# A layer norm's inverse deviations sent through DRAM, two VectorE operations in another form, and a new order of steps

## What is computed

```python
h = concat([tokens(x), txt], axis=1)                 # 64 x 193 x 128
h = h + attention(layernorm(h))                      # group norms, 8 heads, relative positions
h = h + ffn(layernorm(h))                            # 8 experts x 512, two gates per token
# layernorm: (x - mean) / sqrt(var + 1e-5) over the 128 channels
# ffn: top-2 probabilities p of softmax(x @ Wg); sum over i of gelu((x * p_i) @ W1) @ W2, plus biases
```

## Time and profile before

| | before |
|---|---|
| median of 3 runs | 3173.65 us (3173.12 to 3177.37) |
| profiled execution, its own time | 3172.15 us |
| its span, first to last instruction | 3170.3 us |
| TensorE matmul busy | 3053.5 us, 96% of the span |
| VectorE / ScalarE / GpSimd busy | 62% / 59% / 46% |
| TensorE's granted clock | 0.99 of full speed |
| DMA | 38 GB/s over the span |

### The profile page before, as it was taken

The page is one execution under the profiler, slowest core; times in us unless marked ns, Lnnn a source line. Parts: engine busy times, 40 slices in busy tenths (PEclk is TensorE's granted clock), DMA queues, the critical chain, the costliest instruction groups (busy, mean ns, idle before and its releaser), DMA issues.

```text
span 3170.3 us, 61793 instructions
## 1 busy us (share of the span) xinstructions
PE 3053.5 (96%) x19776; PEld 2514.4 (79%) x19776; DVE 1951.6 (62%) x4141; ACT 1873.4 (59%) x4370; POOL 1462.0 (46%) x1350
## 2 busy tenths in 40 slices
PE   6986999999999999999999999999999999999998
PEld 5876888777788888777888887778888877788886
DVE  5634566666666666666666666666666666666665
ACT  4642556665555566655565666555655665555557
POOL 1001445555444445554444455544444555544446
PEclk9998999999999999999999999999999999999999
DMA  9971011111110011111100111111101111111010
GB/s 208 224 200 38 18 26 28 28 27 27 26 28 14 20 28 28 28 26 26 28 20 13 28 28 28 26 28 26 27 6 28 28 28 26 28 26 28 4 26 6
DMA packets 92173, 121.58 MB, mean 38 GB/s; under 512 B 8414, under 2 KB 86558, under 8 KB 87710
## 3 DMA queue, kind: packets, MB, share of 16 engines
q1 hardware_dynamic: 87714, 118.24, 15.9%
q10 hardware_dynamic: 4432, 2.99, 0.4%
HBM read 106.23 MB, written 14.97 MB: 38 GB/s over the span
## 4 chain that ended last, share of the span: by engine, by line
PE 73%; DVE 8%; issue 6%; ACT 5%; DMA 0%; POOL 0%; DVEq 0%; ACTq 0%; POOLq 0%; SPq 0%
PE bank L417 14%; PE bank L517 6%; PE bank L426 6%; PE bank L518 6%; PE bank L562 6%; PE bank L563 6%; PE bank L530 6%; PE bank L430 4%; PE bank L427 4%; PE bank L544 3%; PE bank L462 3%; DVE dl L769 3%; DVE gelu L603 2%; ACT gelu L822 2%; PE bank L572 2%
## 5 line engine op out<-in xcount | busy, mean ns | idle before, releaser
L896 POOL TENSOR_TENSOR gelu<-gelu 128x386 f32<-128x386 f32 x1024 | 1077.1, 1073 | 309.6 <-ACT gelu L823 303.2
L822 ACT ACTIVATE gelu<-bank,b_s 128x386 f32<-128x386 f32 x1024 | 593.9, 580 | 644.4 <-DVE gelu L603 628.5
L417 PE MATMUL bank<-gelu,w_s 128*128 128x386 f32 x2048 | 821.0, 487 | 0.3 <-POOL gelu L896 0.3
L603 DVE TENSOR_TENSOR gelu<-bank,ratio 128x386 f32<-128x386 f32 x1024 | 563.6, 557 | 311.6 <-PE bank L430 308.5
L823 ACT ACTIVATE gelu<-gelu,b_s 128x386 f32<-128x386 f32 x1024 | 625.1, 610 | 0.0
L426 PE MATMUL bank<-x_hi,w_hi 128*128 128x386 f32 x1024 | 544.6, 532 | 19.6 <-ACT gelu L822 8.2
L864 ACT ACTIVATE lp<-bank,mx 128x193 f32<-128x193 f32 x800 | 328.6, 425 | 173.8 <-DVE mx L709 173.4
L517 PE MATMUL bank<-k_f,q_bd 128*128 128x193 f32 x1600 | 402.4, 333 | 15.2 <-DVE a_bd L699 8.7
L518 PE MATMUL bank<-rw,a_bd 128*128 128x193 f32 x1600 | 393.4, 328 | 0.0
L417 PEld LDWEIGHTS bank<-gelu,w_s 128*128 128x128 f32 x2048 | 373.1, 189 | 18.5 <-POOL gelu L896 1.2
L909 POOL TENSOR_TENSOR gst<-gst,half 128x4 f32<-128x4 f32 x32 | 32.6, 1018 | 721.0 <-DVE gst L691 721.0
(11 more groups left out here) (131 smaller groups left out, 4575.4 us busy)
## 6 DMA issues: line engine op xcount, KB each, us to landing
a_rep<-u_scratch SPq DMA_DIRECT2D x32, 1600.0 KB, 9.7
xt<-in_x SPq DMA_DIRECT2D x192, 196.0 KB
txt_s<-in_txt SPq DMA_DIRECT2D x32, 128.0 KB, 2.1
u_scratch<-k_f SPq DMA_DIRECT2D x32, 100.0 KB, 2.2
u_scratch<-q_f SPq DMA_DIRECT2D x32, 100.0 KB, 2.2
out<-o_s SPq DMA_DIRECT2D x64, 48.5 KB
out<-o_s SPq DMA_DIRECT2D x64, 48.0 KB
rv<-in_rel_v SPq DMA_DIRECT2D x1, 2624.0 KB, 14.0
```

The lines of the kernel that those rows point to most:

```text
L417: mm(yb[:, 0:T2], w2_s[:, f, :], gelu1[:, f % RING, :], start=(f == 0), stop=(f == NF - 1)).then_inc(S["w2_done"], 1)
L603: v.tensor_tensor(gelu2[:, f % RING, :], zb[f % 2][:, 0:T2], ratio[:, :], ALU.mult).then_inc(S["z2_done"], 1)
L822: a(gelu1[:, f % RING, :], zb[f % 2][:, 0:T2], ACT.Gelu, bias=b1_s[:, f:f + 1]).then_inc(S["g_done"], 1)
L896: g.tensor_tensor(gelu1[:, f % RING, :], gelu1[:, f % RING, :], gelu2[:, f % RING, :], ALU.add).then_inc(S["hs_done"], 1)
```

## The change

`bc1` on TensorE is gone. SyncE sends the four columns of `rs1` to a row `r_scratch` of 388 numbers in DRAM by four DMAs of 97 or 96 numbers, each number from a partition of its own; it waits for them and reads the row back into all 128 partitions of a new tile `r_bc` by a fifth. VectorE multiplies by `r_bc` instead of the bank. The additions in `gate2` and `hres` become `tensor_tensor` with a broadcast operand in SBUF in place of a constant or a per-partition scalar. `SCHEDULE` is reordered.

```diff
-    "c qs0 c qs1 vt am0 qs2 c log0 am1 am2 log1 log2 qs3 hkeep log3 log4 log5 am3 log6 log7 log8 txt log9 mean1 log10 log11 qs4 var1 log12 c tr0 c bc1 c tr1 inv rel0 tr2 rel1 tr3 rel2 tr4 rel3 tr5 rel4 tr6 rel5 rel6 proj pv0 gmean rec0 pv1 gvar rec1 place0 c place1 c omean gaff c ovar c c c c c nqk c c oaff c c onorm c oh2 c c mean2 c c var2 c top c c gate c gate2 c c bcast w2t w2t xin w2t nv a a w2t ot a otr ocopy hres"
+    "c c vt qs0 am0 qs1 c c qs2 log0 am1 hkeep log1 qs3 log2 am2 txt log3 log4 log5 log6 am3 log7 log8 log9 log10 mean1 log11 log12 c qs4 var1 tr0 c c tr1 inv rel0 tr2 rel1 tr3 bc1 rel2 tr4 rel3 tr5 rel4 tr6 rel5 rel6 proj c pv0 rec0 gmean pv1 rec1 gvar place0 place1 c omean gaff c ovar c c c c c nqk c c oaff c c onorm c oh2 c c mean2 c c nv var2 top c gate c c gate2 c c bcast w2t w2t xin w2t a w2t ot a a otr hres ocopy"
...
-        half = sb("half", [P, 2])
+        half = sb("half", [P, 3])
...
+        r_bc = sb("r_bc", [P, T2])
...
+            def repeat_rstd(t):
+
+                sp.wait_ge(S["rstd1"], t + 1)
+                for k, (a, b) in enumerate(zip(GO, GO[1:] + [T2])):
+                    sp.dma_start(r_scratch[a:b].unsqueeze(1), rs1[0:b - a, k:k + 1]).then_inc(S["r_out"], 16)
+                sp.wait_ge(S["r_out"], t * 64 + 64)
+                sp.dma_start(r_bc[:, :], r_scratch[0:T2].unsqueeze(0).broadcast_to([P, T2])).then_inc(S["rstd_bc1"], 16)
+
             def spread(t):
+                repeat_rstd(t)
...
-                elif s == "bc1":
-                    pe.wait_ge(S["rstd1"], t + 1)
-                    broadcast(misc, rs1).then_inc(S["rstd_bc1"], 1)
...
-                    dve.wait_ge(S["rstd_bc" + k], t + 1)
-                    v.tensor_tensor(V2(sq), V2(delta), ps[:, 0:T2], ALU.mult).then_inc(S["x" + k], 1)
+                    dve.wait_ge(S["rstd_bc" + k], t * 16 + 16)
+                    v.tensor_tensor(V2(sq), V2(delta), r_bc[:, :], ALU.mult).then_inc(S["x" + k], 1)
...
-                    v.tensor_scalar(dl[0:GW, 4:8], ep[0:GW, 0:4], 1.0, None, ALU.add).then_inc(S["e1_ready"], 1)
+                    v.tensor_tensor(dl[0:GW, 4:8], ep[0:GW, 0:4], half[0:GW, 2:3].broadcast_to([GW, 4]), ALU.add).then_inc(S["e1_ready"], 1)
...
-                    v.tensor_scalar(hres[:, :], h2[:, :], b2x2[:, :], None, ALU.add).then_inc(S["hres_done"], 1)
+                    v.tensor_tensor(hres[:, :], h2[:, :], b2x2[:, :].broadcast_to([P, T2]), ALU.add).then_inc(S["hres_done"], 1)
...
+            v.memset(half[:, 2:3], 1.0)
```

More of the change, by code:

```diff
@@ L249, in _, with fused_block @@
                         nc.vector.tensor_copy(xs[0:ROWS, slot, s:s + QS0, :], steps(slot, s, s + QS0)).then_inc(dve_packed, 1)
-def fused_block(nc, txt, w1, tok_scratch, u_scratch, out, R):
+def fused_block(nc, txt, w1, tok_scratch, u_scratch, r_scratch, out, R):
     with ExitStack() as ctx:
@@ L312, in fused_block @@
         names = """w1_in w1_hi_ready w1_split setup_dve setup_pool setup_act tok_in txt_t h_ready qk_ready v_ready
-            bn mv_ready gmean gspread gvar gve grstd affine_part affine norm q_spread a_spread a_masked u_out log_ready max_done log_done
+            bn mv_ready gmean gspread gvar gve grstd affine_part affine norm q_spread a_spread a_masked u_out r_out log_ready max_done log_done
             vt v_copied tr_ready tr0_copied tr1_copied wm_done pv_done pv_ready inv_part inv_ready rec_done o_part obn omv omean ospread ovar ove orstd oaff_part oaffine
@@ L940, in build @@
     u_scratch = nc.dram_tensor("u_scratch", (2, DK, BH, LP), F32, kind="Internal").ap()
+    r_scratch = nc.dram_tensor("r_scratch", (T2 + 2,), F32, kind="Internal").ap()
     with ExitStack() as ctx:
@@ L943, in build @@
         patch_embed(nc, a, tok_scratch, R)
-        fused_block(nc, a["txt"], a["w1"], tok_scratch, u_scratch, out.rearrange("b l c -> (b l) c"), R)
+        fused_block(nc, a["txt"], a["w1"], tok_scratch, u_scratch, r_scratch, out.rearrange("b l c -> (b l) c"), R)
 def shape_constants(np):
```

## The result

| | before | after |
|---|---|---|
| median | 3174.2 us | 3315.8 us (3315.4 to 3319.3) |
| ratio | | 1.0447, 95% interval 1.0429 to 1.0465 |
| span | 3170.3 us | 3313.6 us |
| TensorE busy | 3053.5 us, 96% | 3054.3 us, 92% |
| granted clock | 0.99 | 0.96 |

The change makes the kernel slower by 4.5%. The forecast was 3115 us, range 3085 to 3155: wrong, and on the other side. The rival of the late DMA trip had named the place.

The account below looks back on a forecast made before the run. TensorE was taken to bound the kernel. Terms of -2.05 us per turn over 30 turns (-61.5), -1.5 for first and last turns and +5.6 for the prologue made -57.4 from 3172.15: forecast 3115 us, range 3085 to 3155.

Parts of the forecast that it names:

- The rival of the late DMA trip: At VectorE's bc1: a slower trip of 15.4 us comes 4.9 us late each turn, +152 us, 3267 us; chance 0.14.
- the trip's price: Spreading rs1 through DRAM: write 5.5 us plus read 2.2, sum 7.7, between 6.2 and 9.3, hidden in steady turns.
- The slack: From ready rs1 to VectorE's bc1: trip free up to 8.7 us, costing TensorE nothing up to an estimated 10.5.
- The slower rival: The rival of the late DMA trip, the only one slower than before: 3267 us, chance 0.14.
- the prologue's trip: In the prologue nothing hides the trip: 7.7 us in place of the old spreading's 2.04, +5.6 us once.
- gate2: Addition as tensor_tensor waits for one GpSimd sum, not three: TensorE's wait ahead of bcast goes, -0.80 us per turn.
- The sign that I had named for it: Sign that the gate2 forecast holds: VectorE's addition takes under 1.2 us, the product behind the reciprocal up to 1.1.
- a rival of 0.11: At gate2: the new addition waits as long as the old one, the 0.80 us stays, 3139 us; chance 0.11.
- hres: VectorE's addition as tensor_tensor: 0.56 us alone, up to 0.98 more behind a sum; +0.1 us per turn.
- The order: Reordered SCHEDULE: -0.35 us after var2, -0.39 among the logits, +0.2 for later exponentials and back-to-back place steps, per turn.
- bc1's matmuls: Eight records on TensorE go whole if the numbers return from DRAM in time: -0.81 us per turn.
- the two waits of the tail: TensorE's waits of 0.80 us ahead of bcast and 0.35 after var2, both expected to go each turn.

Follow-up runs that it names:

- e10: Changed kernel with e7's read from other rows and the scratch row's numbers 512 bytes apart in DRAM; norm computed with other numbers: 3084.8 us, a single execution.
- e7: Changed kernel, but the fifth DMA reads different, earlier written rows of another scratch tensor, one per partition; norm computed with other numbers: 3215.7 us, ratio 1.0124.
- e6: Changed kernel with each of the two columns of 97 numbers sent as DMAs of 96 and 1, six writes instead of four: 3246.0 us, ratio 1.0228.
- e1: Changed kernel with bc1 again by TensorE's four matmuls behind tr3, new order and both tensor_tensor forms kept: 3105.8 us, ratio 0.9782.
- e2: Changed kernel with VectorE's bc1 moved from behind tr3 to between rel5 and rel6, DMA trip untouched: 3122.1 us, ratio 0.9832.
- e4: Kernel before with one edit, the addition in gate2 as tensor_tensor: 3174.9 us, ratio 0.9998.
- e5: Kernel before with the new order alone: both additions scalar, bc1 by TensorE's matmuls behind tr3: 3103.6 us, ratio 0.9777.
- e8: Changed kernel with VectorE's bc1 moved from behind tr3 to between tr6 and rel5: 3097.9 us, ratio 0.9755.
- e12: Kernel before with top moved directly behind var2 and one chunk more between gate and gate2: 3171.2 us, ratio 0.9988.

## Why the prediction was wrong

**The failed step is the trip's price.** I wrote 7.7 us, between 6.2 and 9.3, and called it hidden. It took 15.7 in the median and 16.8 in the turn shown. The write leg was put at 5.5 us, between 4.0 and 7.1, and took 9.2 to 13.3, median 10.9. My high end was the output stores, pieces of 512 bytes; I reasoned that smaller pieces could only be faster. e10 shows that the size was not the point: side by side, 4-byte pieces take three times as long as apart. The read leg was put at 2.2 us like any other landing and took 4.8; e7's 2.4 shows that the source is the cause, be it that the row is shared or that it has just been written. The bounds came from rows of transfers that differ in the very properties that counted, so they bounded nothing.

The Trainium skill (DMA: Bandwidth & Descriptors, Specifications) says that below 512 bytes the DMA reads, modifies and writes back. That would make neighbouring 4-byte writes wait for one another and distant ones not; e6 and e10 fit that, but no row shows the read, so it stays an inference.

**The slack was right.** 8.7 us from the ready deviations to VectorE's slot: measured 8.65. For TensorE I allowed a trip of 10.5 us. It ran out of work 12.5 us after the deviations were ready, and VectorE's queued work puts its restart 1.8 us behind the landing (1528.93 to 1530.74), so that a trip of about 10.7 would have cost it nothing.

**The slower rival had the mechanism and lacked the clock.** I gave it 0.14. It put the trip at 15.4 us against the median of 15.7, in part by luck: it took two equal legs of 6.8 us, and they were 10.9 and 4.8. It put TensorE's standstill at 4.9 us per turn; in the 30 steady turns with a trip its waits at L537 come to 5.0 us each. What it had at nothing is the clock. In the turn shown TensorE stands still for 6.2 us and then runs some 4.2 us at half clock, which loses about half of that; less the 0.86 us of matmuls that are gone this makes 7.4 us, an estimate, and the turn is 7.3 us longer than e1's, 95.34 against 88.03. The clock fell to half at every one of these trips.

Spans of after and e1 differ by 209 us. Between the first and the last `bcast` lie 188 of these, 6.3 us in each of the 30 turns that have a trip; the other 21 lie ahead of the first, in the prologue's trip and the first turn's. e2, in which only the prologue's trip is on the path, puts that at 14.8 us, where I had +5.6. With these terms the sum comes out: 3114.8, less 29 for the order and the forms (below), plus 9 for the prologue, 7 for the first turn and 212 for the 30 turns (188, and the 24 of matmuls that I had credited) make 3314 us, against the profiled execution's 3315.4.

**gate2.** Forecast -0.80 us per turn for the form; it brought nothing (e4). The sign that I had named for it, an addition under 1.2 us, came in the changed kernel all the same, and that is luck: the order did it (e5). The Trainium skill's rule (SBUF — State Buffer, "SBUF: two separate sides"), which I set against one row and left to a rival of 0.11, had the edit right: both forms exclude GpSimd alike, and both take 2665 ns in the median here. How long such a wait lasts is for the rows to say: an operation of 0.17 us waited through three sums in a row. I took one instruction's behaviour at one place as a property of its form.

**hres.** +0.1 us forecast; the forms together cost 2.2 us of 3105, 0.07 us per turn (e1 against e5), within what the intervals tell.

**The order.** Forecast for the order and both forms, with `gate2`'s wait and without `bc1`'s matmuls: 0.80 + 0.35 + 0.39 - 0.2 - 0.1 = 1.24 us per turn. Measured: 90.24 - 88.03 = 2.21 (e1), and 90.24 - 87.96 = 2.28 with the scalar forms (e5). The distances between TensorE's starts, in one steady turn of before and one of e5, say where; with a chunk at its usual 1.18 us this is an estimate. From `var2` to `bcast` before took 9.63 us with six chunks and e5 7.29 with five, a gain of 1.16: the two waits of the tail, as forecast. The logits with `txt` and `mean1` took 17.54 against 17.06, a gain of 0.48 where I had 0.39. From `proj` to `omean`, two chunks in both, it was 10.45 against 10.15: a gain of 0.30 where I had charged 0.2. Up to the first logit e5 takes 0.90 us more with one chunk more, a gain of 0.28 where I had none. The rest is spread over the turn.

**bc1's matmuls.** 0.81 forecast, 0.86 measured (e8), once VectorE's product has a place where nobody waits for it.

## What to carry to other kernels

Bound a DMA by rows that share its pattern, not its size: how close together its pieces land in DRAM, and whether it reads one fresh row or many old ones, changed a leg by a factor of two to three here. A trip through DRAM in place of a few matmuls paid here once the consumer stood late enough (e8 against the change: one name moved, 218 us), and it must be kept out of any stretch that nothing covers, such as a prologue. Change one thing at a time before giving it credit: the edit of the form that looked like the gain gave nothing, and the order gave all.

## What the hardware showed unexpectedly

- 386 writes of 4 bytes into one stretch of DRAM, side by side: 9.2 to 13.3 us from the first issue to the fifth DMA's, median 10.9, with DMA share zero for the last 6 in the turn shown; the same 512 bytes apart, 3.6 us in every trip (e10).
- One row of 1544 bytes, just written, read into 128 partitions: 4.8 us; 128 different rows written long before: 2.4 (e7).
- After TensorE had been idle for some 3.5 us its granted clock stood at 0.5 in the turn shown, and the first group of eight matmuls behind the wait took 1.97 us in place of 1.04. The fall can also come once work has begun again: in a turn of the changed kernel with a wait of 3.34 us TensorE resumed at 1243.50, and the clock fell some 1.3 us later.
- VectorE's small additions beside GpSimd's run of sums end with the running sum (0.25 us, e5) or only when the run of sums is over (2.67 us before, 2.8 us in e12). The form does not decide which (e4 and e5); what does is open.
